# Mask products in 64-row halves, new orders of the attention step, and a new start of the expert part

## What is computed

```python
mod = (_silu(L0_c) @ L0_wmod).reshape(8, 6, 1, -1)        # sa, ca, ga, sb, cb, gb
h = _layernorm(x) * (1 + ca) + sa
q, k, v = split(h @ w_qkv)                                  # 16 heads of 16
q = elu(rope(q) * SCALE) + 1;  k = elu(rope(k) * SCALE) + 1
# causal linear attention, token by token
kv = kv + k_t v_t^T;  ks = ks + k_t
out_t = (q_t kv) / max(q_t ks, 1e-6)
x = x + ga * (out @ w_out)
h = _layernorm(x) * (1 + cb) + sb
topv, topi = top_k(softmax(h @ router_w.T), 2)              # 8 experts, two for each token
x = x + gb * sum_e cw[e] * (gelu(h @ w1[e]) @ w2[e])        # 256 -> 1024 -> 256
```

## Time and profile before

| | us |
|---|---|
| median of 3 runs (819.18 to 821.68) | 819.3 |
| the profiled execution | 825.5 |
| span of its trace | 823.2 |
| attention steps in full swing (41.4 to 346.0) | 304.6 |
| routing, between the two parts (about 380 to 415) | 35 |
| expert blocks in full swing (from about 421) | some 400 |

### The profile page before, as it was taken

How to read it: one execution, slowest core, us unless ns; L and a number is a source line. 1 busy time by engine, 2 the same in 40 slices (tenths; PEclk the granted TensorE clock), 3 DMA queues, 4 the chain that set the end, 5 groups by cost and what they waited for, 6 DMA issues and landing times.

```text
span 823.2 us, 26404 instructions
## 1 busy us (share of the span) xinstructions
PE 737.3 (90%) x7949; PEld 540.3 (66%) x7949; DVE 663.8 (81%) x1488; ACT 580.3 (71%) x1103; POOL 514.3 (62%) x504
## 2 busy tenths in 40 slices
PE   6599999999999999973489999999999999999994
PEld 3366666666666666652367777777777777777772
DVE  2789999999999999965857777778777877777773
ACT  1478888888888888862057777777677767677762
POOL 3547576766666575744746666666676667667653
PEclk9799999999999999995589999999999999999998
DMA  6214333333333333310023333343334334343320
GB/s 207 86 41 126 107 115 111 107 108 105 111 113 114 109 116 115 112 53 32 21 79 75 73 71 69 68 78 70 73 73 76 66 69 78 66 76 70 74 31 0
DMA packets 52814, 68.78 MB, mean 84 GB/s; under 512 B 8864, under 2 KB 44080, under 8 KB 52736
## 3 DMA queue, kind: packets, MB, share of 16 engines
q0 software_dynamic: 18176, 27.06, 17.5%
q1 hardware_dynamic: 34560, 40.61, 16.0%
HBM read 46.50 MB, written 22.05 MB: 83 GB/s over the span
## 4 chain that ended last, share of the span: by engine, by line
PE 59%; DVE 16%; issue 10%; ACT 8%; POOL 3%; DMA 1%; DVEq 1%; another core or an unknown queue 0%; ACTq 0%; SPq 0%; POOLq 0%
PE hidden L1334 15%; PE bank L1350 15%; PE hidden L1336 8%; PE bank L1352 7%; PE bank L1189 5%; PE hidden L1172 3%; DVE amlo L511 2%; DVE nb L452 2%; PE bank L1172 2%; ACT feat L969 2%; ACT rb L968 2%; DVE rb L498 2%; DVE hT L475 2%; DVE st L432 2%; ACT qstT L932 1%
## 5 line engine op out<-in xcount | busy, mean ns | idle before, releaser
L1334 PE MATMUL hidden<-qstT,w1hi_k 128*128 128x256 f16 x1136 | 200.2, 274 | 1.1 <-DVE am L723 1.1
L1336 PE MATMUL hidden<-qstT,w1lo_k 128*128 128x128 f16 x1136 | 195.5, 220 | 0.0
L1350 PE MATMUL bank<-w,amhi 128*128 x568 | 188.6, 379 | 0.4
L1352 PE MATMUL bank<-w,amlo 128*128 x568 | 154.8, 273 | 0.0
L729 DVE TENSOR_TENSOR amlo<-am,amhi 128x512 f16<-128x512 f32 x142 | 98.4, 693 | 62.6 <-ACT am L1064 50.8
L919 POOL DMA_INDIRECT out_dram<-x,si x71 | 121.9, 1717 | 36.5 <-issue 27.4
L1334 PEld LDWEIGHTS hidden<-qstT,w1hi_k 128*128 x1136 | 111.7, 98 | 14.9 <-issue 1.3
L1336 PEld LDWEIGHTS hidden<-qstT,w1lo_k 128*128 x1136 | 111.7, 98 | 1.1
L1189 PE MATMUL bank<-wq,hT 128*128 128x256 f32 (+1 forms) x256 | 102.9, 528 | 9.2 <-DVE hT L475 9.1
L1063 ACT ACTIVATE amhi<-am 128x512 f16<-128x512 f32 x142 | 88.5, 623 | 12.6 <-DVE am L723 7.6
L1350 PEld LDWEIGHTS bank<-w,amhi 128*128 128x128 f16 x568 | 55.5, 98 | 62.3 <-issue 2.6
(11 more groups left out here) (203 smaller groups left out, 1814.2 us busy)
## 6 DMA issues: line engine op xcount, KB each, us to landing
stage<-in_L_ffn_w_dram SPq DMA_DIRECT2D x32, 512.0 KB, 4.1
xt<-in_L_attn_x_dram SPq DMA_DIRECT2D x32, 128.0 KB, 2.1
out_dram<-x SPq DMA_DIRECT2D x32, 128.0 KB, 1.7
ffn_rows<-h SPq DMA_DIRECT2D x32, 128.0 KB, 3.3
ffn_rows<-am SPq DMA_DIRECT2D x32, 128.0 KB, 3.1
am<-mod_rows SPq DMA_DIRECT2D x16, 128.0 KB, 3.6
mod_b<-mod_rows SPq DMA_DIRECT2D x8, 256.0 KB, 3.6
w<-in_L_wmod_dram SPq DMA_DIRECT2D x6, 256.0 KB, 4.4
```

The costliest lines, as they stand in the source:

```text
L1334: t.matmul(dst.rearrange("p (q n) -> p q n", q=2), w1s[0][k][g][:, w_], both, start=(k == 0), stop=False)
L1336: last = t.matmul(dst[:, P:2 * P], w1s[1][k][g][:, w_], both[:, 0, :], start=False, stop=(k == KT - 1))
L1350: t.matmul(y[:, :], ghi[:, m.p, c_m], w2s[mt // 2][:, bass.ds(w_, 2 * D)], start=(mt == 0), stop=False)
L1352: last = t.matmul(y[:, D:2 * D], glo[:, m.p, c_m], w2s[mt // 2][:, bass.ds(w_, D)], start=False, stop=(mt == MT - 1))
```

## The change

Four things are changed.

1. **The mask.** Before, a 128 x 128 identity times a 128 x 128 triangle, repeated for four heads, wrote each of the two banks with one product of 128 rows and 512 columns. Now the mask is made of two column halves (late_q 0 and 1), and for each half one product of 64 rows and 256 columns goes to each bank, the one from the upper and the other from the lower 64 rows. POOL builds the two constants at the start with 26 chained operations where there were 16.
2. **The orders.** All five ORDER tuples are new.
3. **The start of the expert part.** The first index column (rows) is copied into gi for five blocks by one operation ahead of the second column, which now has a semaphore of its own (gs); POOL's first shares wait for it. DVE copies the first transposed block before it splits the second block's rows. PE reads all nine words of digits into registers before its first transpose, and does the second block's transpose inside the first block's product, where it stood ahead of it.
4. **Gelu's table** is loaded by a small Gelu ahead of ACT's first row_high.

```diff
-ORDER_PE = (("aT", 4), ("ear", 3), ("pj", 4), ("sc1", 3), ("hT", 0), ("pv0", 3), ("Tk", 2), ("h2T", 6), ("v", 0),
-            ("Tq", 2), ("lg", 6), ("pv1", 3), ("state", 2), ("sc0", 2), ("qk", 0))
+ORDER_PE = (("aT", 4), ("ear", 3), ("sc1", 3), ("pj", 4), ("hT", 0), ("h2T", 6), ("Tk", 2), ("pv0", 3), ("v", 0),
+            ("Tq", 2), ("pv1", 3), ("lg", 6), ("state", 2), ("sc0", 2), ("qk", 0))
...
-ORDER_ACT = (("exp", 2), ("sh0", 3), ("shq", 2), ("sth", 3), ("aTe", 4), ("whi", 1), ("xn", 0), ("xn2", 5),
-             ("sh1", 3), ("kTs", 2), ("h2Te", 6), ("vhi", 0), ("qTs", 2), ("lge", 6))
+ORDER_ACT = (("exp", 2), ("sh0", 3), ("shq", 2), ("sth", 3), ("aTe", 4), ("xn", 0), ("sh1", 3), ("whi", 1),
+             ("kTs", 2), ("xn2", 5), ("vhi", 0), ("h2Te", 6), ("qTs", 2), ("lge", 6))
...
+            dve.wait_ge(s_dve, link.n)
+            v.tensor_copy(gi[:, 0:AHEAD, 0:1], index[:, 0:AHEAD, 0:1]).then_inc(c_["gi"], AHEAD)
             dve.wait_ge(s_pool, POOL_EROW)
...
-            for c in range(AHEAD):
-                load_gi(At(0, c, UC))
+            v.tensor_copy(gi[:, 0:AHEAD, 1:2], index[:, 0:AHEAD, 1:2]).then_inc(c_["gs"], 1)
...
             row_low(At(0, 0, UC))
-            row_low(At(0, 1, UC))
             dve.wait_ge(c_["xT"], 1)
             v.tensor_copy(x16[:, 0, :], bank[0][:, 0:D].bitcast(F16)).then_inc(c_["xTe"], 1)
+            row_low(At(0, 1, UC))
...
+                half = P // 2
+                for u in range(2):
+                    r = slice(u * half, (u + 1) * half)
+                    for late_q in range(2):
+                        link(g.affine_select(out=mask_row[r, late_q, :], in_=mask_row[r, late_q, :],
+                                             compare_op=ALU.not_equal, fill=1.0, base=-half * late_q,
+                                             pattern=[[1, P]], channel_multiplier=-1))
+                    link(g.affine_select(out=later[r, :, :], in_=later[r, :, :], compare_op=ALU.is_ge, fill=MASKED,
+                                         base=0, pattern=[[0, 2], [1, half]], channel_multiplier=-1))
+                    link(g.memset(mask_row[u * half:u * half + 1, 0, 0:half], 0.0))
+                    link(g.memset(mask_row[u * half:u * half + 1, 0, half:P], 1.0))
+                    link(g.memset(later[u * half:u * half + 1, 0, :], MASKED))
...
+                if isinstance(m.n, int) and m.n < AHEAD:
+                    pool.wait_ge(c_["gs"], 1)
...
+            v.activation(st[:, 0, 0:2], minus_half[:, :], ACT.Gelu)
...
-                for odd in range(2):
-                    t.matmul(bank[5 + odd].rearrange("p (h t) -> p h t", t=P), ident_b[:, :],
-                             later[:, :].rearrange("p (u t) -> p u t", u=1).broadcast_to([P, 4, P]),
-                             start=True, stop=False, skip_group_check=True)
+                half = P // 2
+                for late_q in range(2):
+                    for odd in range(2):
+                        r = slice(odd * half, (odd + 1) * half)
+                        t.matmul(bank[5 + odd].rearrange("p (h t) -> p h t", t=P)[:, :, late_q * half:(late_q + 1) * half],
+                                 mask_row[r, late_q, :],
+                                 later[r, late_q, :].rearrange("p (u t) -> p u t", u=1).broadcast_to([half, 4, half]),
+                                 start=(late_q == 0), stop=False, skip_group_check=True)
...
-            xT(At(0, 0, UC))
             pe.wait_ge(s_dve, marks["block_e"])
+            _, words = nc.values_load_multi_w_load_instructions(block_e[0:1, 0:TB // UC], engines=(pe.engine,), min_val=0,
+                                                                max_val=E ** UC - 1)
+            xT(At(0, 0, UC))
...
-                ahead = a.n + UC // 2
-                if ahead % UC == 0 and ahead < MAXB:
-                    load_digits(ahead // UC)
-                if a.back(-1).inside(MAXB):
+                if a.n > 0 and a.back(-1).inside(MAXB):
                     xT(a.back(-1))
...
+                        if a.n == 0 and mt == 3:
+                            xT(a.back(-1))
```

More of the change, by code:

```diff
@@ L58 @@
 Q_SCALE = WS * float(HD ** -0.25)
-ORDER_PE = (("aT", 4), ("ear", 3), ("pj", 4), ("sc1", 3), ("hT", 0), ("pv0", 3), ("Tk", 2), ("h2T", 6), ("v", 0),
-            ("Tq", 2), ("lg", 6), ("pv1", 3), ("state", 2), ("sc0", 2), ("qk", 0))
-ORDER_DVE = (("f", 2), ("st", 0), ("st2", 5), ("mv", 0), ("mv2", 5), ("ve", 0), ("sl0", 3), ("nb", 0), ("rope", 1),
-             ("x1", 4), ("stl", 3), ("hTe", 0), ("sl1", 3), ("wlo", 1), ("den", 3), ("rec", 3), ("vlo", 0), ("at", 3))
-ORDER_POOL = (("shk", 2), ("rs", 0), ("slo", 2), ("R", 1), ("xm2", 5), ("h2", 5), ("wb", 2))
-ORDER_ACT = (("exp", 2), ("sh0", 3), ("shq", 2), ("sth", 3), ("aTe", 4), ("whi", 1), ("xn", 0), ("xn2", 5),
-             ("sh1", 3), ("kTs", 2), ("h2Te", 6), ("vhi", 0), ("qTs", 2), ("lge", 6))
-ORDER_SP = (("ldx", 0), ("ld", 1), ("ro", 6), ("modgb", 6), ("gb", 6), ("modg", 6), ("modb", 7), ("so", 4))
+ORDER_PE = (("aT", 4), ("ear", 3), ("sc1", 3), ("pj", 4), ("hT", 0), ("h2T", 6), ("Tk", 2), ("pv0", 3), ("v", 0),
+            ("Tq", 2), ("pv1", 3), ("lg", 6), ("state", 2), ("sc0", 2), ("qk", 0))
+ORDER_DVE = (("st2", 5), ("st", 0), ("mv2", 5), ("mv", 0), ("ve", 0), ("f", 2), ("sl0", 3), ("nb", 0), ("rope", 1),
+             ("stl", 3), ("x1", 4), ("hTe", 0), ("sl1", 3), ("wlo", 1), ("vlo", 0), ("den", 3), ("rec", 3), ("at", 3))
+ORDER_POOL = (("rs", 0), ("shk", 2), ("slo", 2), ("wb", 2), ("R", 1), ("xm2", 5), ("h2", 5))
+ORDER_ACT = (("exp", 2), ("sh0", 3), ("shq", 2), ("sth", 3), ("aTe", 4), ("xn", 0), ("sh1", 3), ("whi", 1),
+             ("kTs", 2), ("xn2", 5), ("vhi", 0), ("h2Te", 6), ("qTs", 2), ("lge", 6))
+ORDER_SP = (("ldx", 0), ("modg", 6), ("modb", 7), ("so", 6), ("ro", 6), ("ld", 0), ("modgb", 6), ("gb", 6))
 NORM2 = 5
@@ L136, in adaln_block @@
         ident16 = sb("ident16", [P, P], F16)
-        ident_b = sb("ident_b", [P, P], BF16)
-        later = sb("later", [P, P], BF16)
+        mask_row = sb("mask_row", [P, 2, P], BF16)
+        later = sb("later", [P, 2, P // 2], BF16)
         upto = sb("upto", [P, P], F16)
@@ L292, in adaln_block @@
         s_carry = sem("s_carry")
-        c_ = counters("c_", "gi xh xl xT xTe hA hB lA lB sA sB gA gB glA glB y yl ys yw")
+        c_ = counters("c_", "gi gs xh xl xT xTe hA hB lA lB sA sB gA gB glA glB y yl ys yw")
         s_g = [sem(f"s_g{q}") for q in range(GB)]
@@ L384, in carry @@
             eng.sem_inc(s_carry, 1)
-        POOL_CONST = 16
-        POOL_TWO, POOL_EROW = 37, 50
+        POOL_CONST = 26
+        POOL_TWO, POOL_EROW = 47, 60
         POOL_IDENT, POOL_FIRST = 2, 4
@@ L753, in attention_constants @@
                 link(g.memset(ident16[:, :], 0.0))
-                link(g.memset(ident_b[:, :], 0.0))
-                link(g.memset(later[:, :], 0.0))
+                link(g.memset(mask_row[:, :, :], 0.0))
+                link(g.memset(later[:, :, :], 0.0))
                 link(g.memset(v16[:, :, 0, :, HD:VW], 1.0))
@@ L758, in attention_constants @@
                 link(g.memset(state[:, :, :, :], 0.0))
-                for t in (ident16, ident_b):
-                    diagonal(t)
-                for t, fill in ((upto, 0.0), (later, MASKED)):
-                    link(g.affine_select(out=t[:, :], in_=t[:, :], compare_op=ALU.is_ge, fill=fill, base=0,
-                                         pattern=[[1, P]], channel_multiplier=-1))
+                diagonal(ident16)
+                link(g.affine_select(out=upto[:, :], in_=upto[:, :], compare_op=ALU.is_ge, fill=0.0, base=0,
+                                     pattern=[[1, P]], channel_multiplier=-1))
[5 more added lines that the diff above has]
+                                             compare_op=ALU.not_equal, fill=1.0, base=-half * late_q,
+                                             pattern=[[1, P]], channel_multiplier=-1))
+                    link(g.affine_select(out=later[r, :, :], in_=later[r, :, :], compare_op=ALU.is_ge, fill=MASKED,
[3 more added lines that the diff above has]
+                    link(g.memset(later[u * half:u * half + 1, 0, :], MASKED))
                 assert link.n == POOL_CONST, link.n
@@ L1303, in _ @@
             pe.wait_ge(a_["wlo"], NC)
+            pe.wait_ge(s_dve, marks["block_e"])
+            _, words = nc.values_load_multi_w_load_instructions(block_e[0:1, 0:TB // UC], engines=(pe.engine,), min_val=0,
+                                                                max_val=E ** UC - 1)
             xT(At(0, 0, UC))
-            pe.wait_ge(s_dve, marks["block_e"])
-            expert, digits = {}, {}
-            def load_digits(b):
-                digits[b] = pe.value_load(block_e[0:1, b:b + 1], min_val=0, max_val=E ** UC - 1)
-            load_digits(0)
+            expert, digits = {}, dict(enumerate(words))
             def step_c(a):
```

## The result

Each kernel ran four times on one chip: 809.18 us after the change (807.23 to 811.03) and 820.47 before (819.18 to 821.68), a ratio of 0.9862 with an interval of 0.9829 to 0.9896: faster by 1.4%, 11.3 us. The profiled execution took 808.15 us (span 806.3).

A forecast was written before the change was run, and what follows sets the result against it. DVE's round was taken to bound attention steps (10.50 us), PE the expert blocks. Terms sum to -0.35 a step, 10.2 us over 29, plus 1.0 at the expert start: 11.2 off 819.3 gives 808 us; range 796 to 820, forecast's own 803 to 811.

The forecast's parts named there:

- Term 1: Attention step, DVE: nb held only until shk ends, about 0.3 us instead of 0.92; -0.62 a step, bounds -0.77 and 0.
- nb stays behind L829: Rival, attention step: stack_low on POOL starts before amlo is over and still holds nb; step 10.77, 826 us; chance 12%.
- Term 3: Attention step, DVE: features start 1.3 us later beside exp, so their wait for it goes; -0.13 a step.
- Term 4: Attention step, DVE: v's low part, moved ahead, leaves the gap between reciprocal and quotient open; +0.10 a step, bounds 0 and 0.15.
- Term 2: Attention step, DVE: xm2 and h2 both fall on weights_low, 1.87 against 1.57 us; +0.30, bounds -0.28 (no hold) and +1.18.
- The step that failed: Attention step, PE: group's mask falls from 0.43 to 0.21 us, PE's step 9.68 to 9.25, worth nothing by itself.
- the mask's pairs don't overlap: Rival, attention mask: PE stays at 9.68 a step, below 10.15, so the time is the forecast's; no chance given.
- The drain: Attention's end behind 346: same works with long waits for one another; change put at 0, bounds -1.5 and +1.5 us.
- The entry: Start of the expert part: earlier index column and first copy bring the first product sooner; -1.0 us, bounds 0 and -2.
- Gelu's table: 0: Expert part's start, ACT: the 1.28 us table load lies under the second block's first product, so worth 0.
- The nine words: Expert part, PE: their load is covered by idle time before the first transpose; reads within blocks show no gap; 0.
- The start: Kernel's start, POOL: ten more chained operations add 4.3 us, against 3.82 idle; cost 0, bound +0.5 us.

## Why the prediction was right, and where it was not

The sum came out (-11.2 foreseen, -11.3 measured). That it did so within 0.1 us is luck: terms 1 and 3 are right, and the misses of the others cancel.

- *Term 1* (nb no longer behind the low part of the shares, -0.62): right in size, and in cause as far as the runs can tell. Measured (5.7 - 26.8) / 29 = -0.73. The root is held by features, and stack_low starts behind nb. With a root of 0.70, L840 would have started at 244.68 - 0.29 = 244.39, ahead of nb at 244.46 (an estimate from the timeline), and where it does start ahead, nb takes 1.13. But the root's place ahead of shk frees nb too: with features first the root is not held, and nb takes 0.36. By the Trainium skill, "SBUF — State Buffer", Who interferes with whom, the engine that issues first holds the shared port pair for the whole instruction; root (0.70 to 0.99) and nb (0.15 against 0.90) agree. The rival "nb stays behind L829" fell.
- *Term 3* (-0.13, features' wait): right, 3.9 us to 0.2.
- *Term 4* (+0.10, the open gap ahead of the quotient): 0.03; the idle time ahead of the quotient is 1.0 us over 29, and was 0.0.
- *Term 2* (+0.30, weights_low dearer): wrong. (25.9 + 19.2) - (23.1 + 22.3) = -0.3 us, so 0.0 a step. The walk let h be ahead of weights_low; in three steps of four it is behind, and both halves are free, the bound "no hold, -0.28". In the fourth they take 2.37, for wb alone, which the walk left out: the new place of wb costs 6.2 us in the 29 steps, 0.21 a step.
- **The step that failed** is the one on the mask: "On the end this is worth nothing by itself, for PE has room". The first half is true (the mask alone: step 10.50), the reason is not. Room over a step is an average; from amlo through mask, scores and projection to x PE has none once nb no longer holds DVE up. The prediction's walk had no wait ahead of x; there are 10.2 us of it, +0.35 a step, and 18.8 with the old mask. With the old mask the step is 10.49, not the 10.15 that "the mask's pairs don't overlap" gave: by the run with the old mask (822.1, ratio 1.0004) that rival's time would have been that of the kernel before, not the forecast's.
- So the step is -0.73 - 0.13 + 0.03 + 0.35 = -0.48 by the terms and -0.40 by the stretch (the rest is small differences all over DVE's round): near -0.35, because a term that wasn't foreseen (+0.35) took the place of one that was and didn't come (+0.30).
- *The drain* (0, bounds ±1.5): +2.1, outside the bounds. I counted works and their waits there, and not the clock, which is at the lower level for parts of it now. Filling PE's waits gives back 1.5; what is behind the rest is open.
- *The entry* (-1.0): -2.1 for the part alone. Up to the first product it is as said (-0.9 by the trace; the gather's idle time fell from 1.68 to 1.06, where I took 0.5). The rest lies behind it: from the first product to the fifth block's transposes 18.02 us before, 16.86 after. ACT's unnamed wait of 3.98 was a trait of that one execution: with the same entry, the kernels with mask, orders or words alone show 2.4, 2.4 and 2.5 there, and still 18.08, 17.96 and 17.65 to the fifth block. So the gain there is real, 0.5 to 1.2 us, and the trace shows where it lies: in the third block's first product, which takes 3.63, 3.62 and 3.58 us in those three kernels and 2.64 with the change (2.81 with the entry alone), PE being busy all the while. The rows of words alone, and then of the change:

```profile
425.28 0.27 PE L1328 MATMUL hidden<-qstT,w1hi_k 128*128 128x256 f16 x1
...
428.86 0.39 PE L1344 MATMUL bank<-w,amhi 128*128 x1
```

```profile
415.48 0.27 PE L1347 MATMUL hidden<-qstT,w1hi_k 128*128 128x256 f16 x1
...
418.12 0.38 PE L1365 MATMUL bank<-w,amhi 128*128 x1
```

  Why it is slower there is open. Gelu's table no longer stands between ACT's second eviction and the first Gelu (1.9 us from start to start with mask, orders or words alone, 0.49 with the change), but the second product starts no sooner for it: 9.0, 8.9 and 8.6 us behind the first product in those three, 8.8 with the change. No run moved the table alone, so "Gelu's table: 0" is neither confirmed nor refuted.
- *The nine words* (0): 2.1 us for the part alone (interval 0.9 to 3.4), some 1.6 undone. "No gap that could be won" was read off PE's busy time, 249.76 of 250, and there it can't be seen: a matmul's end is modelled in the profile, and lateness hides under it. The starts show it. From the fifth on, blocks start 5.46 us apart in the changed kernel without exception; before, every eighth is up to 0.5 longer, and some others too. PE's timeline of the kernel before, behind the reading of a word, where the next product otherwise starts 0.05 after the L1336 ahead of it:

```profile
440.56 0.27 PE L1334 MATMUL hidden<-qstT,w1hi_k 128*128 128x256 f16 x1
440.67 0.22 PE L1336 MATMUL hidden<-qstT,w1lo_k 128*128 128x128 f16 x1
440.81 0.27 PE L1334 MATMUL hidden<-qstT,w1hi_k 128*128 128x256 f16 x1
...
441.37 0.22 PE L1336 MATMUL hidden<-qstT,w1lo_k 128*128 128x128 f16 x1
441.62 0.39 PE L1350 MATMUL bank<-w,amhi 128*128 x1
```

  0.14 and 0.25 instead of 0.05: the block lasts 5.88. Over all blocks that is 4.7 us in the profiled execution of before, but 0.7 to 1.2 in the four other kernels that read words there. So some 3.5 of the 4.7 us of the expert part were that execution's own, and most of the 5.0 that made it slower than its median; I had rightly put the gain against the median. The words themselves are worth about 1 us by these traces, which both intervals allow.

The start (ten more chained operations; the 26 and 16 are all of POOL's constants, the mask's among them) cost nothing that shows: the first of the stretch's nb starts at 41.39 with the mask alone, and at 41.36 before.

## What to carry to other kernels

Before an operation is called free because its engine has room, lay down the round that will be left once the present stall is gone, and ask who is waited for in it: here a mask that was worth nothing became worth 11 us when the orders changed, and the orders were worth nothing without it, so one of two such edits tried alone proves little. The entry and the words, which no such pair binds, each showed alone what they are worth. Charge a suspected chain at two places with a small, harmless repeat: the place that answers is on it. When a new order is tried, look at the odd step of a round (here one in four, 0.6 to 0.9 us longer) and try to move back what makes it odd.
